# Expert rows on TensorE scaled in place by ScalarE and summed by accumulating transposes

## What is computed

```
z_k  = h . down_embed[index_k]                   (256 numbers)
c_k  = silu(z_k * prob_k)
out  = sum over the 64 picks of c_k * up_embed[index_k]     (512 numbers)
y    = layernorm(x1 + out)
```

## Time and profile before

| | |
|---|---|
| median of 3 runs | 3157.48 us (3154.82 to 3172.02) |
| the profiled execution | 3151.04 us |
| its span (first to last instruction) | 3149.2 us |
| mean granted clock of TensorE | 0.953 of full speed |
| busy, share of span: PE / DVE / ACT / POOL | 89% / 88% / 65% / 65% |
| chain that ended last, by engine | PE 38%, DVE 32%, DMA 9%, POOL 9%, issue 7%, ACT 5% |

### The profile page before, as it was taken

The page is one execution under the profiler, slowest core; times in us unless marked ns, Lnnn a source line. Parts: engine busy times, 40 slices in busy tenths (PEclk is TensorE's granted clock), DMA queues, the critical chain, the costliest instruction groups (busy, mean ns, idle before and its releaser), DMA issues.

```text
span 3149.2 us, 44785 instructions
## 1 busy us (share of the span) xinstructions
PE 2790.8 (89%) x11776; PEld 1737.3 (55%) x11776; DVE 2777.5 (88%) x10160; ACT 2049.7 (65%) x6513; POOL 2062.7 (65%) x2056
## 2 busy tenths in 40 slices
PE   7989899998898999999899989899898999898863
PEld 4565456655555655555566545556555565555541
DVE  3489899998899999999899989999999999899986
ACT  3466766666776666676666676666676666677642
POOL 0066666676676667666667666666766666766676
PEclk9999999999999999999999999999999999999986
DMA  8088888888888888888888888888888888888888
GB/s 284 23 263 275 270 279 273 277 290 282 272 285 265 270 292 287 276 282 277 265 277 297 273 276 271 273 278 290 284 277 268 276 272 288 283 278 281 277 303 272
DMA packets 189855, 856.76 MB, mean 272 GB/s; under 512 B 36192, under 2 KB 39392, under 8 KB 189088
## 3 DMA queue, kind: packets, MB, share of 16 engines
q0 software_dynamic: 163840, 805.44, 77.0%
q1 hardware_dynamic: 19104, 34.87, 3.2%
q10 hardware_dynamic: 6656, 13.60, 1.2%
HBM read 845.38 MB, written 8.39 MB: 271 GB/s over the span
## 4 chain that ended last, share of the span: by engine, by line
PE 38%; DVE 32%; DMA 9%; POOL 9%; issue 7%; ACT 5%; POOLq 0%; SPq 0%; DVEq 0%; ACTq 0%
DVE bank L1143 14%; POOL ring L276 9%; DMA ring<-embed,idx 9%; PE bank L500 8%; DVE ring L1129 8%; PE bank L359 7%; DVE xc L974 6%; PE bank L339 5%; PE bank L441 4%; PE bank L488 4%; PE bank L368 3%; ACT xc L679 1%; PE bank L376 1%; PE bank L307 1%; ACT xskip L691 1%
## 5 line engine op out<-in xcount | busy, mean ns | idle before, releaser
L276 POOL DMA_INDIRECT ring<-embed,idx x2048 | 2061.4, 1007 | 1074.8 <-issue 532.3
L1143 DVE SCALAR_TENSOR_TENSOR bank<-ring,coef,bank 128x512 f32<-128x512 f32 x1312 | 992.4, 756 | 7.4 <-issue 0.2
L1129 DVE SCALAR_TENSOR_TENSOR ring<-ring,hcur 128x256 f32<-128x256 f32 x2048 | 823.8, 423 | 138.5 <-DMA ring<-embed,idx 136.1
L645 ACT ACTIVATE coef<-prob,zp 128x1 f32<-128x1 f32 x2048 | 456.0, 286 | 630.8 <-DVE ring L1129 625.4
L500 PE MATMUL bank<-ring,diag_c 128*128 128x512 f32 x1344 | 672.8, 631 | 115.9 <-ACT diag_c L654 101.3
L463 PE MATMUL bank<-zs,w_up 128*128 128x128 f32 x4096 | 502.2, 287 | 69.2 <-ACT zs L767 65.8
L463 PEld LDWEIGHTS bank<-zs,w_up 128*128 128x128 f32 x4096 | 496.2, 203 | 110.2 <-ACT zs L767 91.8
L500 PEld LDWEIGHTS bank<-ring,diag_c 128*128 128x128 f32 x1344 | 247.2, 199 | 379.2 <-issue 223.7
L974 DVE SCALAR_TENSOR_TENSOR xc<-raw,taps,xc 128x128 f32<-128x128 f32 x960 | 266.2, 351 | 102.6 <-ACT xc L679 102.5
L339 PE MATMUL bank<-w_in,ut 128*128 128x512 f32 (+1 forms) x768 | 285.8, 524 | 4.0 <-ACT seg L667 3.9
L654 ACT ACTIVATE diag_c<-cst,coef 128x128 f32<-128x128 f32 x672 | 234.8, 394 | 48.4 <-PE bank L500 38.0
(11 more groups left out here) (144 smaller groups left out, 3422.2 us busy)
## 6 DMA issues: line engine op xcount, KB each, us to landing
ring<-embed,idx POOLq DMA_INDIRECT x2048, 4.6
ring<-uT SPq DMA_DIRECT2D x4, 2048.0 KB, 14.2
ut<-uT SPq DMA_DIRECT2D x32, 256.0 KB, 6.5
zs<-u SPq DMA_DIRECT2D x32, 256.0 KB, 5.6
out<-acc SPq DMA_DIRECT2D x32, 256.0 KB, 4.6
w_up<-W_upT ACTq DMA_DIRECT2D x1, 4096.0 KB, 13.0
w_in<-W_in ACTq DMA_DIRECT2D x1, 2560.0 KB, 17.4
w_in<-W_in ACTq DMA_DIRECT2D x1, 2048.0 KB, 22.0
```

The source lines that it names most:

```text
L276: pool.indirect_dma_start(out=ring[:, k % RING, :], out_offset=None, in_=embed, in_offset=bass.IndirectOffsetOnAxis(ap=idx[:, half, k:k + ...
L645: m = act.activation(coef[:, k:k + 1], prob_v[:, k:k + 1], ACT.Silu, scale=zp[:, k:k + 1])
L1129: m = dve.scalar_tensor_tensor(out=ring[:, k % RING, 0:DP], in0=ring[:, k % RING, 0:DP], scalar=1.0, in1=hcur[:, :], op0=ALU.mult, op1=ALU ...
L1143: dve.scalar_tensor_tensor(out=total if n == len(DVE_ROWS) - 1 else running[:, :], in0=ring[:, k % RING, DP:ROW], scalar=coef[:, k:k + 1], ...
```

## The change

Of the 64 rows 28 are P and 36 are D: one row more goes to TensorE in each of groups 7, 8, 9, 10 and 12, two in group 11. The diagonal matrices are gone. ScalarE multiplies a P row in place in its ring slot (128x512), and TensorE adds it as 4 transposes of 128x128 that accumulate in `SUM`; the sum stands there transposed. Once a tile ScalarE copies it to `rows_t` (`copy_sum`, after `turn_y`), TensorE transposes it back into bank 0 (`turn_back`, 4 transposes, between `out_proj` and new rows 1 to 3), and `back_sum` waits for that and reads bank 0 (`BACK`). `rows_t` takes the place of `diag_c`. `gated_rms` stands behind the coefficients of group 2, beside the other two square roots. Left out here are the hunks that declare `BACK = 0`, the semaphores `scaled_ok`, `sum_t` and `back_mm`, and put `rows_t` in place of `diag_c` as a buffer of the start.

```diff
@@ -54,8 +54,7 @@
 DTB = 8
 EPS = 1e-5
 BANK = 512
-DIAGS = 4
-GROUPS = ("DD", "PPPD", "DD", "DDD", "PPD", "DDD", "DD", "DDD", "PDDD", "DDD", "DDD", "DDDD", "PDD", "PPPD", "PP", "PDD", "PPPP", "D", "DDD", "PPPD", "D", "PDD")
+GROUPS = ("DD", "PPPD", "DD", "DDD", "PPD", "DDD", "DD", "PDD", "PPDD", "PDD", "PDD", "PPDD", "PPD", "PPPD", "PP", "PDD", "PPPP", "D", "DDD", "PPPD", "D", "PDD")
 NEW = 4
 LAG = 2
 NGRP = len(GROUPS)
@@ -137,7 +136,7 @@
         zp = sb("zp", [P, PICKS])
         raised = sb("raised", [P, EH, TOP])
         coef = sb("coef", [P, PICKS])
-        diag_c = sb("diag_c", [P, DIAGS, P])
+        rows_t = sb("rows_t", [P, KD, P])
         st6b = sb("st6b", [P, 6])
         mvb = sb("mvb", [P, 2])
         smb = sb("smb", [P, 2])
@@ -348,6 +348,8 @@
                         pe.wait_ge(y_ok, 2 * i)
                     else:
                         pe.wait_ge(yT_ok, 2 * i)
+                    if XBC_BANKS[part] == BACK and i >= 3:
+                        pe.wait_ge(sum_ok, 3 * i - 8)
                 for c in range(4 * part, min(4 * part + 4, KC)):
                     m = pe.transpose(bank[XBC_BANKS[part]][:, (c % 4) * P:(c % 4 + 1) * P], seg[:, c, :], ident)
                 m.then_inc(xbc_mm, 1)
@@ -494,13 +496,25 @@
 
                 for k in rows_of(g, "P"):
                     n = PE_ROWS.index(k)
-                    pe.wait_ge(diag_ok, len(PE_ROWS) * t + n + 1)
+                    pe.wait_ge(scaled_ok, len(PE_ROWS) * t + n + 1)
                     if n == 0 and not first:
-                        pe.wait_ge(sum_ok, 3 * t - 2)
-                    m = pe.matmul(bank[SUM][:, :], diag_c[:, (len(PE_ROWS) * t + n) % DIAGS, :], ring[:, k % RING, DP:ROW],
-                                  start=(n == 0), stop=(n == len(PE_ROWS) - 1))
+                        pe.wait_ge(sum_t, t)
+                    for c in range(KD):
+                        m = pe.matmul(bank[SUM][:, c * P:(c + 1) * P], ring[:, k % RING, DP + c * P:DP + (c + 1) * P], ident,
+                                      start=(n == 0 and c == 0), stop=(n == len(PE_ROWS) - 1 and c == KD - 1),
+                                      is_transpose=True, skip_group_check=True)
                 if rows_of(g, "P"):
                     m.then_inc(row_pe, 1)
+
+            def turn_back(t):
+
+                pe.wait_ge(sum_t, t + 1)
+                pe.wait_ge(yT_ok, 2 * min(t + 3, NT))
+                if t > 0:
+                    pe.wait_ge(sum_ok, 3 * t - 2)
+                for c in range(KD):
+                    m = pe.transpose(bank[BACK][:, c * P:(c + 1) * P], rows_t[:, c, :], ident)
+                m.then_inc(back_mm, 1)
 
             def tile(i, first, ahead):
 
@@ -564,6 +578,8 @@
                 new(0)
                 if ahead:
                     out_proj(i + 1, False, 1)
+                if not first:
+                    turn_back(i - 1)
                 new(1, 2, 3)
 
             xbc_proj(0, True, 0)
@@ -597,6 +613,7 @@
             tile(NT - 1, False, False)
             for g in range(NEW, NGRP):
                 weighted(NT - 1, g, False)
+            turn_back(NT - 1)
 
         @block.scalar
         def _(act):
@@ -648,10 +665,15 @@
                 if mine:
                     act.wait_ge(coef_ok, NGRP * t + g + 1)
                 for k in mine:
-                    n = PE_ROWS.index(k)
-                    if len(PE_ROWS) * t + n >= DIAGS:
-                        act.wait_ge(row_pe, NPG * (t - (n < DIAGS)) + signal_of(PE_ROWS[n - DIAGS]))
-                    act.activation(diag_c[:, (len(PE_ROWS) * t + n) % DIAGS, :], ident, ACT.Copy, scale=coef[:, k:k + 1]).then_inc(diag_ok, 1)
+                    act.activation(ring[:, k % RING, DP:ROW], ring[:, k % RING, DP:ROW], ACT.Copy,
+                                   scale=coef[:, k:k + 1]).then_inc(scaled_ok, 1)
+
+            def copy_sum(t):
+
+                act.wait_ge(row_pe, NPG * (t + 1))
+                if t > 0:
+                    act.wait_ge(back_mm, t)
+                act.activation(rows_t[:, :, :], bank[SUM][:, :].rearrange("p (a c) -> p a c", a=KD), ACT.Copy).then_inc(sum_t, 1)
 
             def history(i):
 
@@ -863,11 +885,14 @@
                     state_decay(i + 1, range(NH // 2))
                     state_decay(i + 1, range(NH // 2, NH))
                     turn_y(i + 1)
+                if not first:
+                    copy_sum(i - 1)
                 new(0, 1)
                 if ahead:
                     gated_squares(i + 1)
+                new(2)
+                if ahead:
                     gated_rms(i + 1)
-                new(2)
                 if not first:
                     back_sqrt(i - 1)
                 if ahead:
@@ -902,6 +927,7 @@
             tile(NT - 1, False, False)
             for g in range(NEW, NGRP):
                 coefs(NT - 1, g)
+            copy_sum(NT - 1)
             back_sqrt(NT - 1)
 
         @block.vector
@@ -1170,8 +1196,8 @@
 
             def back_sum(t):
                 dve.wait_ge(row_used, len(DVE_ROWS) * (t + 1))
-                dve.wait_ge(row_pe, NPG * (t + 1))
-                dve.tensor_tensor(total, total, bank[SUM][:, :], ALU.add).then_inc(sum_ok, 1)
+                dve.wait_ge(back_mm, t + 1)
+                dve.tensor_tensor(total, total, bank[BACK][:, :], ALU.add).then_inc(sum_ok, 1)
                 dve.wait_ge(sum_ok, 3 * t + 1)
                 dve.bn_stats(st6b[:, :], total).then_inc(sum_ok, 1)
                 dve.wait_ge(sum_ok, 3 * t + 2)
```

More of the change, by code:

```diff
@@ L163, in build @@
         Y_BANKS, ST_BANKS, YT_BANKS, OP, XBC_BANKS = (6, 7), (4, 1), (2, 0), 6, (7, 2, 0)
-        X1T, UP_BANKS, DOWN, HT, SIM_BANKS, SUM = 6, (4, 1, 7, 2), 6, 6, (7, 6), 5
+        X1T, UP_BANKS, DOWN, HT, SIM_BANKS, SUM, BACK = 6, (4, 1, 7, 2), 6, 6, (7, 6), 5, 0
         running = bank[3]
@@ L178, in build @@
         soft_buf = {0: [acc[:, 0, n * P:(n + 1) * P] for n in range(3)],
-                    1: [acc[:, 0, 0:3 * P], acc[:, 1, 0:3 * P], diag_c[:, 0:3, :].rearrange("p a b -> p (a b)")]}
+                    1: [acc[:, 0, 0:3 * P], acc[:, 1, 0:3 * P], rows_t[:, 0:3, :].rearrange("p a b -> p (a b)")]}
         soft_tiles = {0: slice(0, DTB), 1: slice(DTB, NT)}
@@ L201, in build @@
         xr_mm, xr_ok, skip_ok = sem("xr_mm"), sem("xr_ok"), sem("skip_ok")
-        yT_ok, sq_ok, rms_ok, ln_ok, x1T_ok, h1_ok, hT_ok, exp_ok, hcur_ok, coef_ok, diag_ok, ln2_ok, saved_ok = (
+        yT_ok, sq_ok, rms_ok, ln_ok, x1T_ok, h1_ok, hT_ok, exp_ok, hcur_ok, coef_ok, scaled_ok, ln2_ok, saved_ok = (
             sem(n) for n in ("yT_ok", "sq_ok", "rms_ok", "ln_ok", "x1T_ok", "h1_ok", "hT_ok", "exp_ok", "hcur_ok",
-                             "coef_ok", "diag_ok", "ln2_ok", "saved_ok"))
+                             "coef_ok", "scaled_ok", "ln2_ok", "saved_ok"))
+        sum_t, back_mm = sem("sum_t"), sem("back_mm")
         cur_ok, conv_ok, cbm_ok, xdt_ok, g_ok, xdec_ok, yoff_ok, y_half, y_ok, dcy_ok, st_ok, rr_ok, bn_ok, x1_ok, h_ok = (
```

## The result

The changed kernel takes **3345.04 us** (median of 4 runs, 3340.96 to 3352.67) against 3156.15 us for the kernel of before beside it: ratio 1.0595, 95% interval 1.056 to 1.0629. It is slower, as forecast, but by 6% where 2.8% was forecast, and outside the range, whose end was 3300.

What follows compares the result with a forecast made beforehand. PE and DVE, both busy nearly nine tenths, bound it together along a chain; 1.5 + 0.7 + 1.0 + 0 + 0.7 - 1.0 = +2.9 us a tile, times 30 = +87, plus 2, gave 3240, forecast 3244 us; range 3115 to 3300.

Steps and rivals of the forecast that it cites:

- gate to transposes, with the clock: DVE's gate to `xbc_proj`'s transposes: `back_sum` +1.5, two scalings before the bank copy +0.7, low clock after PE's idle +1.0 us.
- transposes to `up_proj`: From `xbc_proj`'s transposes to `up_proj`, ACT's chain: 0, since group 5 has no P row.
- `up_proj` to h: PE's five P rows instead of one add 1.4 us, DVE's mean lateness of 0.7 is gained: +0.7 us a tile.
- h to the gate: From h to DVE's next gate: three additions less save 2.0, PE's rows before `key_scores` add 0.9: -1.0 us a tile.
- TensorE's own rows before h: Between `up_proj` and h, five P rows by transposes instead of one by diagonal: +1.4 us a tile (0 to 1.8).
- its lateness at h: DVE's mean lateness when PE waits for h before `turn_h`: 0.7 us a tile, to be gained as PE alone decides.
- The scalings: On ACT, 28 scalings replace 21 diagonals, slot 0.65 us against 0.30; group 16's four put 1.4 us ahead of `end_decay`.
- The transposes: On PE, a transpose's slot is 0.109 us, so four make 0.44 us a P row against 0.86 by diagonal.
- The square roots: On ACT, moving `gated_rms` beside the other square roots saves two table loads a tile, without effect.
- VectorE sets the tile: Rival, chance 0.15: 4.6 us of additions go, 1.5 of new wait come back, -3.1 us a tile, 3066 us.
- Its own sign: Sign for the VectorE rival: PE still waits over 0.5 us for h in the changed kernel.
- TensorE's clock sinks over the new rows: Rival, chance 0.10: two more clock drops a tile on PE's stretches, +96 us, 3340 us; sign, mean clock below 0.93.

Runs made afterwards that it cites:

- the three mends: Changed kernel with `back_sum` behind `residual`, `xbc_proj` part 2 in bank 0, group 4's scalings behind the first bank copy: with 28 P rows 3566 us, second kind of session.
- the mended kernel: Changed kernel with the three mends and the 21 P rows of before: 3113.9 us, ratio 0.9867 to the kernel of before, first kind of session.
- f1_serve7: Against the 28-row kernel with the three mends (3566 us), TensorE serves group 7 right behind `up_proj` part 0: 3521 us, ratio 0.969.
- f2_ring12: Changed kernel with 12 ring slots instead of 13: 3784 us, ratio 1.041, second kind of session.

## Why the prediction was wrong

The direction and the first link were right; the size wasn't. By its steps, in us a tile (medians from the table, total +7.2; the mean by the pick numbers is +6.4):

| step | forecast | measured | difference of means |
|---|---|---|---|
| gate to transposes, with the clock | +3.2 | 26.50 - 22.09 = +4.4 | +3.9 |
| transposes to `up_proj` | 0 | 5.96 - 5.60 = +0.4 | +0.3 |
| `up_proj` to h | +0.7 | 25.97 - 24.10 = +1.9 | +1.7 |
| h to the gate | -1.0 | 41.84 - 41.27 = +0.6 | +0.8 |

**The step that failed is "h to the gate: -1.0", and with it "`up_proj` to h: +0.7".** Both took VectorE's saved additions as time that it would have, bounded by PE alone. But a row handed to TensorE keeps its slot until TensorE comes to it. VectorE works two groups behind its dot products, TensorE only between blocks of up to 12 us. The term for TensorE's own rows before h was right (+1.4 forecast, 24.5 - 23.3 = +1.2 measured to the end of `down_proj`). What failed is VectorE's side of it: its lateness at h, 0.7 us, was to vanish and grew by 0.5. From h to the gate the sum closes with the wait that was left out: the mean of before, 41.6, less the 2.0 us of additions, plus 4.1 - 2.0 = 2.1 us more for gathered rows and 0.4 for the key scores is 42.1, and 42.4 was measured. So the seven rows cost more than they free. At 21 P rows the two steps measured 24.10 and 40.45: 0 and -0.8. The forecast put the seven rows' whole effect there at -0.3 us a tile (0.7 - 1.0, but for the diagonals' share of it); taking them away brought 112 / 30 = 3.7 us, half of it TensorE's work. The prediction named the waits for gathered rows (3.4 us a tile) and left them as they were; GpSimd's own waits on TensorE, 240.9 us, stood in the rows of before and weren't asked. More than 13 slots weren't tried. Apart from this, the last sum of the forecast is off by two: 3240 + 6.4 is 3246, not 3244.

**"Gate to transposes: +2.2 us, and the clock"**: the mechanism was right, two terms were small. `back_sum` came 2.0 us later, not 1.5, since `out_proj` ended 0.3 us later and not 0.3 earlier: it starts earlier, but takes 8.2 in place of 7.6 us, in the low clock behind a longer wait for the gate. The bank copy was 2.7 us later (2.2 forecast). The idle was 3.5 us (3.2), and part 2 took 3.57 us in place of 1.83 in the median tile, all of it at 0.50: +1.75 where +1.0 was taken of a bound of 2.1. On the mean it is 3.1 in place of 1.8, +1.3, as the clock held in some tiles. The 119 us that the three mends bring at 21 rows aren't the price of this step alone: they put the transposes at 20.70, 1.4 us ahead of where they were before the change.

**The scalings.** 714 ns each and a slot of (2.56 - 0.71) / 3 = 0.62 us, 0.65 taken: right, and the estimate from the Trainium skill ("ScalarE: Activation LUTs", what ACT_TABLE_LOAD costs) was 0.61. What was underrated is group 16, four scalings in a row: the forecast saw them only as a delay of `end_decay`, but TensorE waits for them 71.9 / 24 = 3.0 us a tile, ahead of `y_diag`, and then works in the low clock in most tiles. It waited 37.3 / 26 = 1.4 us for the diagonals before. It waits as long at 21 rows, where h to the gate is still 0.8 us shorter than before, so this isn't what made that step longer.

**The transposes** have the slot forecast: (1782.34 - 1781.03) / 12 = 0.109 us. The square roots had no effect that could be measured, as forecast.

**The rivals.** *VectorE sets the tile* is out: seven additions less and 189 us more. Its own sign did show (PE waits 41.3 / 24 = 1.7 us for h, over 0.5), and it misled: VectorE loses 3.5 us a tile for want of rows between `up_proj` and `down_proj`'s end. It isn't the whole of that wait, since with 21 P rows, where VectorE lacks no rows there, PE waits 2.0 us: VectorE then has its additions back and starts behind the same late copy. *TensorE's clock sinks over the new rows* comes nearest in its time (3340 us) and fits the mean clock (0.907, under the 0.93 asked for), but the rows give the fall another cause. Every low stretch between 500 and 2900 us, 44 before and 84 after, begins in an idle of TensorE of over 0.8 us or at most 4.7 us behind its end. The stretches add up to 164 us before and 410 after. With 21 P rows they are 331, and in the mended kernel 280, 113 of them behind the wait for group 16. The idle in `xbc_proj` had 113 of the 410 behind it, and has none there. The rule that transposes don't count as busy ("TensorE: Matmul & The Clock Gate", Part 4, of the Trainium skill) isn't needed for any row here, nor is it refuted: no run has the transposes without the idles. Two things speak for it: behind the same idle before part 2 the clock held in 3 of 24 tiles with 28 P rows and in 9 of 25 with 21, and the mended kernel's clock, 0.94 over 500 to 2900 us, is still below the 0.97 of before. The clock adds to a wait here: before part 2, 3.5 us of idle brought 1.3 us of slower work behind it on the mean.

**Open** are the share of each of the three mends in the first kind of session, what they would bring to the kernel of before, and the cause of the idle stretches in the second kind. `f1_serve7` and `f2_ring12`, on which the slot theory rests beside the traces, were run in the second kind only.

## What to carry to other kernels

Before work is moved from a busy engine to a free one, ask how long the new owner holds the buffer. In a ring of gathered rows the slot is the price: an engine that comes by only between long blocks holds it for longer than the work takes, and the starved engine is the one that was relieved. A new step that an in-order engine waits for is put behind whatever doesn't need it (`back_sum` behind `residual`). With that, the bank and the scalings mended and the rows as they were, the kernel with transposes is 1.3% faster than before where the change lost 6%.

## What the runs showed of the hardware

- Two kinds of sessions: 3157 and about 3640 us for the same kernel, the latter with idle stretches on all engines that no event in the profile ends. They hid a loss of 6% (ratio 1.0595 in the first kind, 0.989 in the second). A verdict from one kind needn't hold in the other.
- A float32 transpose of 128x128 adds into a bank at 0.109 us a slot, as a plain one does, so a scaled row costs TensorE 0.44 us in place of 0.86 by a diagonal matrix.
- Behind an idle of 3.35 to 3.6 us the 8 matmuls of `xbc_proj` part 2 took 3.57 us at a granted clock of 0.50 in 12 of 24 tiles, and 1.83 us in three. On the mean they took 3.1 us in place of 1.8, so the idle costs 3.5 + 1.3 us.
